# Third attention: keys, values and scores as three products of high and low parts, its weights and context loaded in slices

## The reference, cut to what matters

```python
H, HD = (16, 64)
q = jnp.einsum('bsf,fhd->bshd', inputs_q, Wq) + bq      # inputs_q = layernorm(x)
k = jnp.einsum('bsf,fhd->bshd', inputs_k, Wk) + bk      # inputs_k = inputs_v = context
v = jnp.einsum('bsf,fhd->bshd', inputs_v, Wv) + bv
q = q / jnp.sqrt(jnp.asarray(depth, q.dtype))
attn = jnp.einsum('bqhd,bkhd->bhqk', q, k)
attn = jax.nn.softmax(attn, axis=-1)
x = jnp.einsum('bhqk,bkhd->bqhd', attn, v)
out = jnp.einsum('bqhd,hdo->bqo', x, Wo) + bo
```

## Time and profile before

| | |
|---|---|
| median of 3 runs | 1836.31 us (1836.01 to 1838.53) |
| the profiled execution | 1832.85 us, span 1831.1 us |
| PE / PEld busy | 1664.6 us (91%) / 1050.0 us |
| DVE / ACT / POOL busy | 1058.6 / 867.5 / 227.9 us |
| mean granted clock | 0.965 |
| first score of the third attention | 1014.43 us |
| its last pair of steps starts | 1608.79 us |

### The profile page before, as it was taken

How to read it: one execution, slowest core, us unless ns; L and a number is a source line. 1 busy time by engine, 2 the same in 40 slices (tenths; PEclk the granted TensorE clock), 3 DMA queues, 4 the chain that set the end, 5 groups by cost and what they waited for, 6 DMA issues and landing times.

```text
span 1831.1 us, 31330 instructions
## 1 busy us (share of the span) xinstructions
PE 1664.6 (91%) x10800; PEld 1050.0 (57%) x10801; DVE 1058.6 (58%) x2899; ACT 867.5 (47%) x2022; POOL 227.9 (12%) x294
## 2 busy tenths in 40 slices
PE   4898989988888786999999799999999999998998
PEld 1555555533333375999997344454455455457887
DVE  3677677655556364222222787665665665667776
ACT  2788888635555412443343466655544654530000
POOL 0111111103441211111111330000000000010000
PEclk8999999889999877999999799999999999999999
DMA  7687778300000190111114200000000000020001
GB/s 267 238 288 265 275 252 291 118 1 1 1 1 1 65 375 24 35 37 37 34 37 132 84 27 4 20 1 1 0 1 1 1 1 1 12 81 1 1 0 46
DMA packets 55403, 140.11 MB, mean 77 GB/s; under 512 B 5904, under 2 KB 32400, under 8 KB 50800
## 3 DMA queue, kind: packets, MB, share of 16 engines
q1 hardware_dynamic: 51872, 129.20, 20.6%
q0 software_dynamic: 3408, 9.31, 1.8%
HBM read 87.25 MB, written 51.25 MB: 76 GB/s over the span
## 4 chain that ended last, share of the span: by engine, by line
PE 78%; DVE 10%; ACT 7%; issue 4%; DMA 1%; SPq 0%; POOL 0%; DVEq 0%; ACTq 0%; POOLq 0%
PE PS L699 14%; PE PS L1238 9%; PE PS L1102 8%; PE PS L1087 7%; PE PS L1193 6%; PE PS L1183 5%; PE PS L1208 5%; PE PS L906 4%; PE PS L766 3%; PE PS L788 3%; PE PS L1169 3%; PE PS L926 2%; PE PS L799 2%; ACT PTf L1520 1%; ACT P L1611 1%
## 5 line engine op out<-in xcount | busy, mean ns | idle before, releaser
L1611 ACT ACTIVATE P<-PS,nm 128x512 f32<-128x512 f32 x256 | 172.6, 687 | 193.5 <-DVE nm L2173 193.5
L1193 PEld LDWEIGHTS PS<-idf,P 128*128 128x128 f32 x1024 | 113.3, 141 | 97.9 <-issue 80.1
L1882 DVE CUSTOM_DVE_ANT_0 dump<-PS,maskw 128x256 f32<-128x256 f32 (+3 forms) x256 | 114.8, 488 | 92.2 <-PE PS L911 87.0
L2173 DVE TENSOR_REDUCE nm<-PS 128x2 f32<-128x1024 f32 x128 | 150.6, 1218 | 26.5 <-PE PS L1183 26.4
L1793 DVE CUSTOM_DVE_ANT_0 SN<-PS,SR 128x128 f32<-128x128 f32 (+3 forms) x256 | 115.2, 488 | 83.8 <-PE PS L770 83.6
L1102 PEld LDWEIGHTS PS<-xT,W1c 128*128 128x128 f32 x1248 | 148.2, 195 | 4.4 <-ACT xT L1573 2.4
L1102 PE MATMUL PS<-xT,W1c 128*128 128x128 f32 x1248 | 148.8, 278 | 1.8 <-ACT xT L1573 1.8
L1193 PE MATMUL PS<-idf,P 128*128 128x128 f32 x1024 | 138.7, 277 | 12.7 <-ACT PTb L1620 8.7
L1087 PE MATMUL PS<-EW,hT 128*128 x624 | 141.2, 379 | 0.0
L906 PE MATMUL PS<-QP,KP 32*128 32x128 f32 (+3 forms) x512 | 107.6, 493 | 36.6 <-ACT PTf L1520 33.4
L1520 ACT ACTIVATE PTf<-PS 128x512 f32<-128x512 f32 (+3 forms) x256 | 97.9, 435 | 82.7 <-PE PS L906 82.5
(11 more groups left out here) (259 smaller groups left out, 2957.6 us busy)
## 6 DMA issues: line engine op xcount, KB each, us to landing
SR<-rel SPq DMA_DIRECT2D x16, 1024.0 KB, 7.4
rel<-EN SPq DMA_DIRECT2D x15, 1024.0 KB, 4.8
SR<-rel SPq DMA_DIRECT2D x16, 768.0 KB, 6.2
rel<-EN SPq DMA_DIRECT2D x15, 768.0 KB, 4.3
SR<-rel SPq DMA_DIRECT2D x16, 512.0 KB, 4.4
EW<-in_fc1T SPq DMA_DIRECT2D x8, 1024.0 KB, 12.9
EW<-in_fc2T SPq DMA_DIRECT2D x8, 1024.0 KB, 12.9
rel<-EN SPq DMA_DIRECT2D x15, 512.0 KB, 3.4
```

The source lines that it names most:

```text
L1193: last = nc.tensor.transpose(TR1[j][:, c * P:c * P + P], P1[s % 4][:, j, c * P:c * P + P], idf[:])
L1611: last = af(P1[s % 4][:, j, :], PD[s % 2][:, j, :], ACT.Exp, bias=nm1[:, s % 4, j:j + 1], accum_out=sm1[:, s % 4, j:j + 1])
L2173: v.tensor_reduce(nm1[:, s % 4, :], PD[s % 2][:], AX.X, ALU.max, negate=True).then_inc(c_max, 1)
```

## The change

It computes keys, values and scores of the third attention each as three fp32r products: high by high, high by low, low by high, where high is the fp32r rounding of an f32 operand and low the rest. For weights and context ACT writes the high part and POOL subtracts it to get the low part; for keys and queries of a block DVE writes the high part and POOL the low part. The query projection stays in f32. To make room, the weights lie in slices for one block (keys, queries) or four blocks (values) and the context in two buffers of one sequence; SP loads each slice anew when its buffer is free. POOL's list is rewritten: the indirect DMAs of sequences 1, 2 and 3 stand at the head of blocks 0, 1 and 3, and the bias additions in blocks 8 to 11. A few semaphores are merged (`wk0` into `ctx0`, the router's four into two).

```diff
+            def context_of(b):
+                sp.dma_start(CT[b % 2][2][:], context[:, :, b * S:b * S + S]).then_inc(ld["ctx1" if b % 2 else "ctx1_0"], 16)
+
+            def weights_of(name, p, n):
+                return A[name].rearrange("(k p) n -> p k n", p=P)[:, :, p * P:(p + n) * P]
+
+            def key_query_weights(m):
+                p = m % HP
+                sp.dma_start(WK[m % 2][2][:], weights_of("wk1", p, 1)).then_inc(ld["wkq1" if m % 2 else "wkq0"], 16)
+                sp.dma_start(WQ[m % 2][:], weights_of("wq1", p, 1)).then_inc(ld["wkq1" if m % 2 else "wkq0"], 16)
+
+            def value_weights(g):
+                sp.dma_start(WV[2][:], weights_of("wv1", g * VG % HP, VG)).then_inc(ld["wv1"], 16)
...
-            sp.dma_start(WO1[:], A["wo1"].rearrange("(k p) n -> p k n", p=P)).then_inc(ld["wo1"], 16)
+            context_of(1)
+            for m in range(NC1 - 2):
+                sp.wait_ge(c_gw, G_AT["q", m] + 1 if m else G_AT["q", 0, 1] + 1)
+                key_query_weights(m + 2)
+                if m % HP == HP - 1 and m // HP + 2 < B:
+                    context_of(m // HP + 2)
+                if m % VG == 1 and m // VG + 1 < NC1 // VG:
+                    sp.wait_ge(c_gw, G_AT["v", m // VG * RT + RT - 1] + 1)
+                    value_weights(m // VG + 1)
+                if m == HP:
+                    sp.wait_ge(ln_sem[3]["var"], B + 1)
...
+            def low_part(parts):
+                high, low, full = parts
+                nc.gpsimd.tensor_tensor(low[:], full[:], high[:].bitcast(F32), ALU.subtract).then_inc(c_low, 1)
+
+            def weights_low(use):
+                kind, i = use
+                pool.wait_ge(c_wh, WH_AT[use] + 1)
+                low_part(WK[i % 2] if kind == "wk" else WV if kind == "wv" else CT[i % 2])
+
+            def keys_low(m):
+                pool.wait_ge(c_rh, RH_AT["k", m] + 1)
+                low_part((KH[m % 2], KL[m % 2], K1[m % 2]))
+
...
+            for use in (("ct", 0), ("wk", 0), ("wk", 1), ("wv", 0)):
+                weights_low(use)
+            keys_low(0)
+            pool.wait_ge(s_e["idx"], 2)
+            for s in range(2):
+                pool.wait_ge(s_yst[s], 16 * ((NT0 + 1 - s) // 2))
+            for tb in range(RT):
+                gather(tb)
+            keys_low(1)
+            for x in range(2):
+                first_queries_low(x)
             pool.wait_ge(ld["rows1"], 32)
-            for tb in range(TB):
-                pool.wait_ge(ln_sem[3]["nrm"], tb + 1)
-                nc.gpsimd.tensor_tensor(X[:, tb], X[:, tb], rows1[:, H1 * DH1:], ALU.add).then_inc(s_xb, 1)
+            for m in range(NC1):
+                if m in (0, 1, 3):
+                    pool.wait_ge(c_nat, max(2, RT * m + 1))
+                    for r in range(RT):
+                        gather(RT * ((m + 1) // 2 + 1) + r)
+                if m + 1 < NC1:
+                    if m:
+                        keys_low(m + 1)
+                    queries_low(m + 1)
+                for use in _weight_splits(m):
+                    weights_low(use)
+                for tb in range(RT * (m - HP), RT * (m - HP + 1)):
+                    if 0 <= tb < TB:
...
+            def project_parts(bank, w, src):
+
+                terms = [(h, x, k) for h, x in ((0, 0), (1, 0), (0, 1)) for k in range(DK)]
+                for h, x, k in terms:
+                    last = mm(bank[:], w(h, k), src(x, k), start=((h, x, k) == terms[0]), stop=((h, x, k) == terms[-1]))
+                return last
+
...
-                              start=True, stop=True)
+                terms = [(QH, KH), (QL, KH), (QH, KL)]
+                for n, (q, k) in enumerate(terms):
+                    for j in range(2):
+                        o = DH1 * j
+                        last = mm(PD[s % 2][:, j, :], q[m % 2][o:o + DH1, r * P:r * P + P], k[m % 2][o:o + DH1, :],
+                                  start=(n == 0), stop=(n == len(terms) - 1))
                 last.then_inc(c_nat, 1)
...
+            def context_high(b):
+                act.wait_ge(ld["ctx1" if b % 2 else "ctx1_0"], 16 * (b // 2 + 1))
+                af(CT[b % 2][0][:], CT[b % 2][2][:], ACT.Copy).then_inc(c_wh, 1)
...
+                if r == 2:
+                    for use in _weight_splits(m):
+                        weights_high(use)
...
+            def keys_high(m):
+                dve.wait_ge(c_gr, G_AT["k", m] + 1)
+                v.tensor_scalar(KH[m % 2][:], K1[m % 2][:], 1.0, None, ALU.mult).then_inc(c_rh, 1)
...
+            def queries_high(m):
+                dve.wait_ge(c_gr, G_AT["q", m] + 1)
+                v.tensor_scalar(QH[m % 2][:], Q1[m % 2][:], 1.0, None, ALU.mult).then_inc(c_rh, 1)
...
+                    if r == 0 and m + 1 < NC1:
+                        if m:
+                            keys_high(m + 1)
+                        queries_high(m + 1)
```

More of the change, by code:

```diff
@@ L164, with _weight_splits @@
 N_G = len(C_USES)
+def _weight_splits(m):
+    uses = [("wk", m + 2)] * (m + 2 < NC1) + [("wv", m // VG + 1)] * (m % VG == 1 and m // VG + 1 < NC1 // VG)
+    return uses + [("ct", m // HP + 1)] * (m % HP == 2 and m // HP + 1 < B)
+LOWS = [("ct", 0), ("wk", 0), ("wk", 1), ("wv", 0), ("k", 0), ("k", 1), ("q", 0, 0), ("q", 0, 1)]
+for _m in range(NC1):
+    LOWS += [("k", _m + 1)] * (0 < _m < NC1 - 1) + [("q", _m + 1)] * (_m < NC1 - 1) + _weight_splits(_m)
+LOW_AT = {_use: _i for _i, _use in enumerate(LOWS)}
+WH_AT = {_use: _i for _i, _use in enumerate([_use for _use in LOWS if _use[0] not in "kq"])}
+RH_AT = {_use: _i for _i, _use in enumerate([_use for _use in LOWS if _use[0] in "kq"])}
 AT_OUT = [NST + RT + 7 + RT * _w for _w in range(7)]
@@ L565, in _ @@
                     store_outputs(2 * jp + s, s)
[L566 removed]
+            context_of(0)
             store_outputs(last_tile(3), 0)
[L568 to L571, removed]
+            for m in range(2):
+                key_query_weights(m)
+            value_weights(0)
+            for j in range(last_tile(3) + 1, NT0):
                 store_outputs(j, j % 2)
[L573 to L574 removed]
             for s in range(2):
@@ L1154, in values_to_bank @@
                 b, p = divmod(g * VG, HP)
[L1155 to L1160, removed]
+                pe.wait_ge(c_low, max(LOW_AT["wv", g], LOW_AT["ct", b]) + 1)
+                project_parts(bank1(("v", i)) if bank is None else bank, lambda h, k: CT[b % 2][h][:, k, c * P:c * P + P],
+                              lambda h, k: WV[h][:, k, :]).then_inc(c_gw, 1)
             def project_out(i):
@@ L1596, in _, with key_weights_high, value_weights_high, weights_high @@
                     moe0_tile(2 * jp + s, s)
+            def context_high(b):
+                act.wait_ge(ld["ctx1" if b % 2 else "ctx1_0"], 16 * (b // 2 + 1))
+                af(CT[b % 2][0][:], CT[b % 2][2][:], ACT.Copy).then_inc(c_wh, 1)
+            def key_weights_high(m):
+                act.wait_ge(ld["wkq1" if m % 2 else "wkq0"], 32 * (m // 2 + 1))
+                af(WK[m % 2][0][:], WK[m % 2][2][:], ACT.Copy).then_inc(c_wh, 1)
+            def value_weights_high(g):
+                act.wait_ge(ld["wv1"], 16 * (g + 1))
+                af(WV[0][:], WV[2][:], ACT.Copy).then_inc(c_wh, 1)
+            def weights_high(use):
+                kind, i = use
+                if kind == "wk":
+                    key_weights_high(i)
+                elif kind == "wv":
+                    value_weights_high(i)
+                else:
+                    context_high(i)
             moe0_tile(NT0 - 3, 0)
+            context_high(0)
+            key_weights_high(0)
             moe0_tile(NT0 - 2, 1)
+            key_weights_high(1)
+            value_weights_high(0)
             moe0_tile(NT0 - 1, 0, last=True)
```

90 lines of the change are left out of this document (49 added, 41 removed).

## The result

The changed kernel took 1862.6 us, median of 4 (1859.16 to 1866.16), beside 1837.42 of before, median of 4 (1836.01 to 1848.57): a ratio of 1.0119, interval 1.0092 to 1.0146. Slower, as forecast, and the whole interval lies above 1, but by far more: +25.2 us between these medians, where +6.3 us was the sum, 1842.6 the time and 1856 the end of the range. The profiled execution took 1861.58 us.

What follows compares the result with a forecast made beforehand. PE sets the pace of the long part, DVE is nearly as full early, and the start is a chain of waits. -17.3 + 0 + 18.7 + 5.5 - 0.6 = +6.3 on 1832.85: 1839.2, median 1842.6, range 1828 to 1856.

Steps and rivals of the forecast that it cites:

- start, to block 1: Before block 1's scores: they wait for POOL's second eight DMAs and the queries' low part; +5.5 us, ends 2 and 8.
- first pairs at -0.72: Key and query pairs, blocks 7 to 30: keys and scores each save 0.36 us on PE; 24 pairs, -17.3.
- second pairs at 0: Blocks 7 to 30: DVE's high parts delay the maxima (nm), cancelling PE's saving; sum 0, ends -3 and +3 for 24 pairs.
- 5 x 3.2: Second pairs of blocks 2 to 6: combine and POOL's subtractions take turns, maxima (nm) at about 5.4 us; +3.2 each.
- 0.8: Second pair of block 1: POOL first issues eight DMAs, so the combine slips through; +0.8 us.
- 1.5: First pairs of blocks 1 to 6, where low parts of weight slices meet a combine; +1.5 us.
- -0.7: First pairs of blocks 1 to 6 gain only where DVE's chain doesn't carry its delay on; -0.7 us in all.
- half of the -0.7 for value chunks: Second value chunks in blocks 4 and 8 were forecast to save 0.7 us together.
- The ends that the prediction gives: Bounds: early part +4 if DVE always wins the turn, +24 if POOL does; start 2 and 8 us.
- Rivals 3 and 4: Scores' weight loads show, +38, 1880; or 64-row fp32r products go one at a time, 1894; chance 0.05 each.
- The 0.07: First pairs: PE's path to the second transposes, 5.72, stays 0.07 us behind the maxima's chain, 5.65; the pair takes 8.57.
- second transposes = the later of PE's path and nm + 4.65: Pairs that aren't light: second transposes start at PE's own path or 4.65 us after the maxima (nm) start, whichever is later.

Runs made afterwards that it cites:

- Experiment 4: Changed kernel with the high parts of keys and queries made by ACT instead of DVE (all but the first two of keys): 1836.53 us, ratio 0.9996.
- Experiment 3: Changed kernel with POOL's subtractions of keys and queries cut to 16 columns, scores using the high parts three times: 1843.87 us, ratio 1.0016.
- experiment 6: Changed kernel with DVE's combine of first pairs moved ahead of its copy of the queries in blocks 1 to 6: 1847.81 us, ratio 1.0041.
- experiment 5: The kernel before, unchanged, traced a second time: 1841.26 us, one execution, beside a median of 1841.08.
- experiment 7: Changed kernel with ACT making the high parts of keys and queries and the first pairs' combine ahead of the queries' copy: 1828.6 us, ratio 0.9926.
- experiment 8: Changed kernel with scores in f32 in blocks 0 to 7, in parts from block 8, high parts made by ACT: 1829.18 us, ratio 0.9937.
- experiment 1: Changed kernel with scores in f32, without high and low parts of keys and queries; key and value projections stay in parts: 1829.8 us, ratio 0.9944.
- 2: Changed kernel with the key and value projections in f32 from the sliced loads, scores still in parts: 1874.4 us, ratio 1.019.

## Why the prediction was wrong in its size

The direction and most mechanisms were right; the sum was +6.3 and the trace shows +20.4 against the second trace of before. The step that failed is the second pairs of the long part, priced at 0 by a formula that lacked a wait; the early blocks were too small beside it. By its own terms:

| term | forecast | measured |
|---|---|---|
| start, to block 1 | +5.5 | +1.9 |
| blocks 1 to 6 | +17.2 | +22.7 |
| blocks 7, 8 | 0 | +2.4 |
| blocks 9 to 30 | -15.8 | -6.7 |
| rest | -0.6 | +0.1 |

(The forecast's first pairs at -0.72 and second pairs at 0 are laid out over these stretches; its 5 x 3.2, 0.8, 1.5, -0.7 and half of the -0.7 for value chunks are blocks 1 to 6. In blocks 9 to 30, first pairs had -15.8 and gained 11.9, second pairs had 0 and lost 5.2. The ends that the prediction gives for the early part and the start lead to 1850.4, with the second pairs' +3 to 1853.4; no term leads to the 1856 of its range, and 1862.6 is above all of them.)

**First pairs: right, but for 3.9 us.** 8.64 us against 8.57, nm at 1.00, scores of 1.59 against 1.56. Rivals 3 and 4 are out: no weight load shows, and 64-row fp32r products overlap. The 0.07 makes 1.5 us. Two of the 22 pairs (blocks 14 and 22), in which a normalisation meets the subtraction of WV (1.50 us instead of 0.41), take 9.05, which the prediction had at no cost, and one took 10.23 at a lower clock.

**Second pairs: the step that failed most.** The prediction took "second transposes = the later of PE's path and nm + 4.65" for the whole rule and priced the later nm at 0 for 24 pairs. That rule held (4.65 measured). What it left out is that the *next* further product needs the same bank: it starts at nm + 6.06 to 6.15, behind DVE's copy of V. In the kernel before, with nm at 1.18, this would be 7.32, just ahead of the 7.38 of PE's own path, so nothing could be seen of it. With nm at 1.44 (1.66 was forecast) it is 7.5 to 7.6 and with statistics 7.92, while PE's own path had become shorter. By kinds (v a value chunk, o the output projection, n, m and g the short ones): v,o 11.54 against 11.10, v,n 8.09 against 7.97, v,g 9.39 against 9.27, v,v,o 14.04 against 13.86; a lone "n" behind a normalisation, which is bound by nm itself, 8.20 against 7.54; only the pairs that put the projection first (8.80 against 9.14) and v,v (9.15 against 9.30) gained. Experiment 4 takes the delay of nm away and gets 9.9 us back in second pairs, the 5.2 lost and 4.6 of gain. The formula's part was off as well, but the other way: where no statistics stand ahead, nm came 0.22 sooner than forecast. I had asked what comes second after nm and not what comes last.

**Early blocks: right mechanism, too small by 5.** nm at 4.73 to 5.76 us in five of the six second pairs (5.4 forecast), halves of the combine of 1.50 and 1.38 us: the turns are as forecast, though not which block escapes. That is block 3 (nm at 2.98), where KL started at 1095.63, behind POOL's eight DMAs and after the combine (1092.21). Experiment 3 prices them at 12.3 us, experiment 6 at 14.7 together with the place of the combine. Under-priced were block 1, which I spared with 0.8 and which pays 4.1 (nm at 5.76, 11.26 us against 7.20; the second half of its combine took 3.20 us, through both subtractions), and block 6's first pair, where the low part of WV makes a normalisation take 2.45 us and nm comes at 4.72 (13.79 against 10.10). I also took PE's work at the full clock: the granted clock is 0.88 over the 131.5 us, and behind some of the idle stretches products run at half speed for a while. How much of the 22.7 us is the clock's was not measured by itself. The Trainium skill says, in "SBUF — State Buffer", section "SBUF: two separate sides", that the ports which VectorE and GpSimd share go as a lock to one of them for a whole instruction (VectorE wants them with two inputs in SBUF or in a two-port mode), and the later one stands until it ends. The traces agree: 1.50 us for a combine's half beside a subtraction of 1.39, 0.48 without one, and nm, which reads PSUM, undisturbed.

**Blocks 7, 8.** The second pair of block 8 has two normalisations behind QH. Each met a subtraction (1.36 us instead of 0.41); I had let one of them do so. 14.24 us against 10.89; experiment 4 has 10.55.

**Start: too large by 3.6.** The mechanism is there as forecast (eight DMAs, then QL, then the scores, rows above), but the DMAs began at 1028.37, which is 1023.4 on the first trace's scale, and not at 1025.7. Q of the second half is no later than before (1026.61 with the lag of 4.9 in it, 1022.06 in the first trace), and QH and QL put 1.8 us behind it, where I had 3.6. PE idled 2.50 us ahead of the scores of block 1, where I had over 3. Block 0 as a whole takes 18.9 us, as it did (18.4).

**Rest.** Costs nothing; the +3 that it shows against the first trace is variation (experiment 5), and so is the +4.9 ahead of the change. The prediction tied itself to one trace and corrected by 3.5 us for its median; the medians of before in the later comparisons were 1837.4, 1838.9 and 1841.1.

## What to carry to other kernels

When an operation is put ahead of one that others wait for, follow every chain from it to the end of the period, through each buffer that exists once, and not only to the first consumer; a chain that ties with the bound leaves no row in the profile, and the saving elsewhere uncovers it. Put such conversions on the engine that waits anyway (here ACT, 0.63 us before its maxima arrive), and put DVE's combines and normalisations, which read and write SBUF, into a stretch in which it idles, away from POOL's. Judge the parts of a change apart: here one half was a gain of half a per cent and the other a loss of nearly two. And trace the old kernel twice before differences of 3 to 5 us outside the change are explained, and compare the granted clock pair by pair before two gains are said not to add up.

## What the runs showed of the hardware

- ACT writes a 128x512 fp32r copy in 0.63 us, DVE in 0.42 (0.33 from start to start), where the nearest row of before had 0.48.
- The granted clock also fell where PE had not idled. In the changed kernel the first pair of block 16 takes 10.23 us instead of 8.64; the pair ahead of it had PE busy 8.52 of 9.00 us at 1.00. The windows:

```profile
1336.00:1345.00 9.00, 8.52 (x60) 5.80 (x56) 6.58 (x13) 4.66 (x12) 3.35 (x3) 1.00 0.11 32
1345.00:1355.20 10.20, 10.20 (x47) 5.45 (x46) 5.35 (x10) 5.53 (x13) 0.00 (x0) 0.83 0.00 0
```

  It fell in the same pair in experiments 3, 6, 7 and 8 and in none of 1, 2 and 4, nor in the kernel before; in 7 and 8 it fell in the first pair of block 22 too. Why there stays open; in block 16 it is worth 1.6 us.
- After an idle wait of 2.16 us four records of the queries' product took 3.55 us instead of 1.98, at a granted 0.53, the lower level of 1.2 GHz. PE and the window in experiment 7:

```profile
1106.74 1.07 PE L1278 MATMUL PS<-idf,P 128*128 128x128 f32 x8 [2.16 <-ACT PTb L1730]
1107.65 3.55 PE L785 MATMUL PS<-NT,WQ 128*128 128x512 f32 x4
```

```profile
1107.60:1111.20 3.60, 3.60 (x8) 1.06 (x6) 1.19 (x3) 1.90 (x4) 1.26 (x1) 0.53 0.00 0
```

  An idle wait alone does not explain it. Experiments 1 and 8 run the same code in the first pair of block 6 and wait as long there, 3.16 us. In experiment 1 the clock stays at 1.00, in experiment 8 it is 0.50 behind the wait. Experiment 1, then 8:

```profile
1135.42 1.06 PE L1270 MATMUL PS<-idf,P 128*128 128x128 f32 x8 [3.16 <-ACT PTb L1722]
1136.32 1.88 PE L777 MATMUL PS<-NT,WQ 128*128 128x512 f32 x4
```

```profile
1142.76 1.94 PE L1274 MATMUL PS<-idf,P 128*128 128x128 f32 x8 [3.16 <-ACT PTb L1726]
1144.49 3.62 PE L781 MATMUL PS<-NT,WQ 128*128 128x512 f32 x4
```

- Two executions of the kernel before differ by 4.9 us at the end of the first expert layer, and the other kernels lag 3.0 to 12.8 us behind the first of them; nearly all of it arises in the first attention (there the second trace of before falls back by 5.05 us), which the change touches only in the semaphore of one load (wk0).
